# Two small float32 products of a fused attention and feed-forward kernel run as three passes of split operands

## The reference, cut to what matters

```python
z = x + x @ W.T + b            # for q, k1, k2, v1, v2, then split into 16 heads of 8
S1 = k1.T @ v1 / n ; S2 = k2.T @ v2 / n        # per batch and head, 8 x 8
out = (q @ S1 * mean(v2)) * g1 + rowsum(S1*S2) * g2 + (q @ S2 * mean(v1)) * g3 + (q @ (S1*S2)) * g4
x = layernorm(x + layernorm(out) @ Wo.T + bo)
x = layernorm(x + ffn_norm(x + relu(x @ w1 + b1) @ w2 + b2))
```

## Time and profile before

| what | value |
| --- | --- |
| median of 3 runs | 205.26 us (204.93 to 206.01) |
| profiled execution, its own time | 204.86 us |
| span of the profiled execution | 203.1 us |
| TensorE busy in the span | 191.3 us, 94% |
| VectorE busy | 157.7 us, 78% |
| GpSimd busy | 136.3 us, 67% |
| ScalarE busy | 129.2 us, 64% |
| mean granted TensorE clock | 0.991 of full speed |

### The profile page before, as it was taken

One profiled execution on the slowest core, in us unless ns is written; L12 is line 12 of the kernel. 1 busy time (PEld: TensorE's weight loads), 2 busy tenths in 40 slices (PEclk: granted clock), 3 DMA queues, 4 the chain that ended last, 5 costly groups with the idle time before them and its releaser, 6 DMA issues.

```text
span 203.1 us, 4279 instructions
## 1 busy us (share of the span) xinstructions
PE 191.3 (94%) x1375; PEld 174.7 (86%) x1375; DVE 157.7 (78%) x471; ACT 129.2 (64%) x386; POOL 136.3 (67%) x176
## 2 busy tenths in 40 slices
PE   6899999999999999999999999999999999999920
PEld 6788997999898999999997989898989899987820
DVE  0186745987879887898879896989698969897683
ACT  0342538373759665975858685967597759786852
POOL 8526670476489838986598759885988598877350
PEclk9999999999999999999999999999999999999996
DMA  5999501200001100101001400100010101011012
GB/s 149 247 230 283 154 0 32 52 0 5 0 0 52 48 6 2 56 0 52 3 14 50 118 4 0 53 24 31 2 52 5 52 3 52 2 52 38 17 53 103
DMA packets 12625, 10.64 MB, mean 52 GB/s; under 512 B 714, under 2 KB 10459, under 8 KB 12603
## 3 DMA queue, kind: packets, MB, share of 16 engines
q1 hardware_dynamic: 11944, 9.32, 15.3%
q0 software_dynamic: 352, 0.92, 2.4%
q10 hardware_dynamic: 306, 0.13, 0.2%
HBM read 6.17 MB, written 4.20 MB: 51 GB/s over the span
## 4 chain that ended last, share of the span: by engine, by line
PE 83%; DVE 6%; issue 3%; DMA 2%; ACT 2%; POOL 2%; DVEq 0%; POOLq 0%; SPq 0%; ACTq 0%
PE down_ps L997 25%; PE up_ps L997 24%; PE z_ps L997 14%; PE prep_ps L997 12%; PE turn_ps L1144 4%; PE turn_ps L1115 3%; DMA X<-in_L_attn_x 2%; DVE st L766 1%; DVE down_ps L817 1%; POOL y L528 1%; POOL y2g L524 1%; DVE z_ps L877 1%; DVE y2n L773 1%; ACT res L640 1%; DVE res L974 0%
## 5 line engine op out<-in xcount | busy, mean ns | idle before, releaser
L997 PE MATMUL down_ps<-w_sb,hT 128*128 128x128 f32 x480 | 58.9, 276 | 0.1
L997 PEld LDWEIGHTS down_ps<-w_sb,hT 128*128 128x128 f32 x480 | 56.4, 192 | 0.7 <-ACT hT L658 0.3
L658 ACT ACTIVATE hT<-up_ps,cols 128x512 f32<-128x512 f32 x64 | 42.3, 682 | 5.0 <-PE up_ps L997 4.7
L640 ACT ACTIVATE res<-y,nb,rstd 128x128 f32<-128x128 f32 x60 | 24.8, 483 | 6.6 <-POOL nb L510 5.9
L550 POOL TENSOR_TENSOR x1b<-x,b_rows 128x512 f32<-128x512 f32 x16 | 20.6, 1287 | 11.8 <-DVE x L773 11.8
L997 PE MATMUL up_ps<-x1T_hi,w_hi 128*128 128x512 f32 x64 | 26.1, 408 | 0.0
L997 PE MATMUL up_ps<-x1T_lo,w_hi 128*128 128x512 f32 x64 | 25.4, 398 | 0.0
L997 PE MATMUL up_ps<-x1T_hi,w_lo 128*128 128x512 f32 x64 | 25.3, 395 | 0.0
L524 POOL TENSOR_TENSOR y2g<-y2n,gamma_rows 128x512 f32<-128x512 f32 x15 | 19.3, 1285 | 8.1 <-DVE y2n L773 8.1
L773 DVE TENSOR_SCALAR x<-z_ps,st,rstd 128x128 f32<-128x128 f32 x64 | 21.9, 405 | 0.1
L607 ACT ACTIVATE z_sq<-z_ps 128x128 f32<-128x128 f32 x64 | 16.8, 270 | 8.1 <-PE z_ps L997 8.1
(11 more groups left out here) (160 smaller groups left out, 408.9 us busy)
## 6 DMA issues: line engine op xcount, KB each, us to landing
X<-in_L_attn_x SPq DMA_DIRECT2D x8, 512.0 KB, 8.8
out<-res SPq DMA_DIRECT2D x15, 256.0 KB, 2.0
V_all<-V_dram SPq DMA_DIRECT2D x6, 128.0 KB, 3.2
w_sb<-in_L_ffn_w POOLq DMA_DIRECT2D x2, 256.0 KB, 8.3
out<-res SPq DMA_DIRECT2D x2, 128.0 KB, 2.2
w_raw<-in_L_attn_Wv ACTq DMA_DIRECT2D x2, 64.0 KB, 2.6
w_raw<-in_L_attn_Wk SPq DMA_DIRECT2D x2, 64.0 KB, 3.8
w_raw<-in_L_attn_Wo POOLq DMA_DIRECT2D x1, 64.0 KB, 3.0
```

The lines of the kernel that those rows point to most:

```text
L640: last = act.activation(res[buf][:, t, :], y3[buf][:, t, :], ACT.Identity, scale=rstd4[:, t:t + 1], bias=nb4[:, t:t + 1])
L658: act.activation(hT[:, k, :], up_ps[k % len(up_ps)][:, :], ACT.Relu, bias=cols[:, 5 + k:6 + k]).then_inc(relu_out, 1)
L997: return pe.matmul(o, lhsT, rhs, start=start, stop=stop)
```

## The change

For batches 2 to 7 `gram_av` and `centered` no longer multiply float32 operands. Each operand is split into a high part in fp32r and its remainder in fp32r, and the product is the sum of high times high, high times low and low times high, three fp32r matmuls in one accumulation. So `gram_av(b)` has three matmul instructions where it had two, and `centered(b)` has six where it had four.

The constant sides are split once by GpSimd at the start of step 0 (`split_A`, `split_both`, two operations of 128 x 256 each). G of each batch is split by GpSimd at the end of the even steps 0 to 10, one step and more ahead of its use (`split_G`, two operations of 128 x 128). The high part of PT is what ScalarE's `PT_copy` now writes. The remainder is a new VectorE subtraction, `PT_rest`, that stands between the second and the third tile of x1 and waits for `PT_out`. `centered` waits for it (`PTlo_out`) before its first matmul.

```diff
@@ gpsimd
+            def split_both():
+                pool.wait_ge(zw_ready, 1)
+                pool.tensor_copy(both_hi[:, :, :], center[:, :, :]).then_inc(both_split, 1)
+                pool.wait_ge(both_split, 1)
+                pool.tensor_tensor(both_lo[:, :, :], center[:, :, :], both_hi[:, :, :].bitcast(f32), ALU.subtract).then_inc(both_split, 1)
+            def split_A():
+                pool.wait_ge(A_ready, 1)
+                pool.tensor_copy(A_hi[:, :, :], A_kv[:, 0:2, :]).then_inc(A_split, 1)
+                pool.wait_ge(A_split, 1)
+                pool.tensor_tensor(A_lo[:, :, :], A_kv[:, 0:2, :], A_hi[:, :, :].bitcast(f32), ALU.subtract).then_inc(A_split, 1)
+            def split_G(b):
+                g, k = b % 2, 2 * (b - 2)
+                pool.wait_ge(G_out, b + 1)
+                wait(pool, ev_done, b - 1)
+                pool.tensor_copy(G_hi[:, g, :], G_sb[:, b, 0:C]).then_inc(G_split, 1)
+                pool.wait_ge(G_split, k + 1)
+                pool.tensor_tensor(G_lo[:, g, :], G_sb[:, b, 0:C], G_hi[:, g, :].bitcast(f32), ALU.subtract).then_inc(G_split, 1)
             def body(st):
+                if st.n == 0:
+                    split_A()
+                    split_both()
...
+                if st.cur and n % 2 == 0 and n // 2 + 2 < BATCHES:
+                    split_G(n // 2 + 2)
@@ scalar, PT_copy
-                act.activation(PT_sb[:, :], prep_ps[:, 0:XW], ACT.Copy).then_inc(PT_out, 1)
+                act.activation(PT_sb[:, :] if b < 2 else PT_hi[:, :], prep_ps[:, 0:XW], ACT.Copy).then_inc(PT_out, 1)
@@ vector
+            def PT_rest(b):
+                wait(dve, PT_out, b + 1)
+                dve.tensor_tensor(PT_lo[:, :], prep_ps[:, 0:XW], PT_hi[:, :].bitcast(f32), ALU.subtract).then_inc(PTlo_out, 1)
-                    normalize(x1, y1_tile, st2, rstd2, x1_out)
+                    normalize(x1, y1_tile, st2, rstd2, x1_out, (lambda: PT_rest(st.prepared())) if st.prep and n >= 0 else None)
@@ tensor, gram_av, b >= 2
-                    mm(prep_ps[:, 0:256], G_sb[:, b, 0:C], A_kv[:, 0:2, :].rearrange("p j c -> p (j c)")).then_inc(ev_done, 1)
+                    if b == 2:
+                        pe.wait_ge(A_split, 2)
+                    wait(pe, G_split, 2 * (b - 1))
+                    hi, lo = (t[:, :, :].rearrange("p j c -> p (j c)") for t in (A_hi, A_lo))
+                    mm(prep_ps[:, 0:256], G_hi[:, b % 2, :], hi, start=True, stop=False)
+                    mm(prep_ps[:, 0:256], G_hi[:, b % 2, :], lo, start=False, stop=False)
+                    mm(prep_ps[:, 0:256], G_lo[:, b % 2, :], hi, start=False, stop=True).then_inc(ev_done, 1)
@@ tensor, centered
+                if b >= 2:
+                    wait(pe, PTlo_out, b - 1)
+                    pe.wait_ge(both_split, 2)
+                    hi, lo = (t[:, :, :].rearrange("p j c -> p (j c)") for t in (both_hi, both_lo))
+                    for part, pt in ((slice(0, 256), lambda t: t[:, 0:C]),
+                                     (slice(256, 512), lambda t: t[:, C:C + 1].to_broadcast([128, 128]))):
+                        mm(prep_ps[:, part], pt(PT_hi), hi, start=True, stop=False)
+                        mm(prep_ps[:, part], pt(PT_hi), lo, start=False, stop=False)
+                        last = mm(prep_ps[:, part], pt(PT_lo), hi, start=False, stop=True)
+                    last.then_inc(p_done, 1)
+                    return
```

More of the change, by code:

```diff
@@ L77, in build @@
         A_kv = sb("A_kv", [128, 5, 128])
+        A_hi = sb("A_hi", [128, 2, 128], f32r)
+        A_lo = sb("A_lo", [128, 2, 128], f32r)
+        G_hi = sb("G_hi", [128, 2, 128], f32r)
+        G_lo = sb("G_lo", [128, 2, 128], f32r)
         WoT = sb("WoT", [128, 128])
@@ L119, in build @@
         PT_sb = sb("PT_sb", [128, XW])
+        PT_hi = sb("PT_hi", [128, XW], f32r)
+        PT_lo = sb("PT_lo", [128, XW], f32r)
+        both_hi = sb("both_hi", [128, 2, 128], f32r)
+        both_lo = sb("both_lo", [128, 2, 128], f32r)
         PQ_hi = sb("PQ_hi", [128, 512], f32r)
@@ L227, in build @@
         rows_done = sem("rows_done")
+        both_split = sem("both_split")
+        PTlo_out = sem("PTlo_out")
+        A_split = sem("A_split")
+        G_split = sem("G_split")
         rows_out = sem("rows_out")
```

## The result

| | before | after |
| --- | --- | --- |
| median | 205.21 us (21 runs) | 205.68 us (21 runs) |
| ratio | | 1.0023, 95% interval 1.0014 to 1.0032 |
| span of the profiled execution | 203.1 us | 204.2 us |

The changed kernel is 0.47 us slower (0.29 to 0.66 by the interval). The forecast was 206.0 us, with "no change" as the likeliest class. The granted clock is the same in both profiles, 0.991 before and 0.992 after.

A forecast was written before the change was run, and what follows sets the result against it. TensorE's chain was taken as the bound: 1.02 us lost at `centered` (six times 0.17) less 0.24 saved at the product with G gives +0.78 us, 206.0 us on the median; range 204.7 to 207.0 us.

The forecast's parts named there:

- no change: Whole kernel: a time within about 0.5% (1.03 us) of before, between 204.2 and 206.3 us; chance 0.62.
- TensorE's chain is the bound, and `centered` starts the moment its input is there: At `centered`: its first load follows ScalarE's copy by 0.05 us, so waiting for PT_lo loses TensorE 0.33 us per batch.
- The rival that the wait is hidden: At `centered`: the remainder costs TensorE nothing, 1.2 us saved, 204.1 us; chance 0.12.
- The subtraction takes 0.30 us: `PT_rest` on VectorE: 130 columns take 0.30 us, by a line through 256 and 512 columns; bounds 0.16 and 0.425 us.
- the dearer remainder: Rival at `PT_rest`: the subtraction costs as much as one of 256 columns, 206.8 us; chance 0.18.
- the even case: Rival at `centered`: `PT_rest` takes near 0.16 us, so wait and saving even out, 205.2 us; chance 0.10.
- Three fp32r matmuls of 256 columns cost 0.354 us, six 0.71: Both products, at 0.118 us per matmul: `gram_av` saves 0.08 us per batch, `centered` 0.16 against float32's 0.87.
- the rival of slow spread loads: At `centered`: three matmuls loading the spread PT column cost 0.49 us more per batch, 208.9 us; chance 0.08.
- the estimate from the Trainium skill's four passes for true FP32: Both products: three passes cost three quarters of float32, saving 0.11 and 0.22 us per batch, sum +0.33 us; not adopted.
- the sum from the rows: Whole kernel: 1.02 us lost at `centered` less 0.24 saved at the product with G, +0.78 us.
- G's saving reaches the end in three batches of six: At `gram_av`: 0.08 us saved in batches 2 to 4, 0.24 in all; waits absorb it in 5 to 7.
- GpSimd hides its splits, VectorE's later x1 costs nothing: GpSimd's splits fit its idle gaps; x1's late tiles keep 1.3 us of cover, without which 0.5 us per batch.

The follow-up runs named there:

- the two kernels: Kernel before with only the subtraction and TensorE's wait added, all products float32: 207.33 us; changed kernel with the product with G back in float32: 206.01 us.
- the two halves of the change: Changed kernel with only the centered product split, 206.01 us, and with only the product with G split, 204.88 us.
- two pairs of kernels: Product with G split against float32: the changed kernel, 205.68 against 206.01 us; the kernel before, 204.88 against 205.30 us.
- rest_unwaited: Kernel before with the unread VectorE subtraction added and PT in its own bank, TensorE not waiting for the subtraction: 204.87 us, ratio 0.9986.
- rest_twice: Changed kernel with the subtraction done twice in a row on VectorE, the first into an unread tile: 206.81 us, 1.0077 of the kernel before.

## Why the prediction was right, step by step

*TensorE's chain is the bound, and `centered` starts the moment its input is there.* Right. The wait sits where it was put, and its 0.33 us per batch was measured by itself as 2.03 us in six batches. The rival that the wait is hidden is out: the load waits for PT_lo in all six batches, 0.33 to 0.34 us each.

*The subtraction takes 0.30 us.* The group rows of the kernel after, by form (busy us, mean ns, idle before):

```profile
L832 DVE TENSOR_TENSOR PT_lo<-prep_ps,PT_hi 128x130 fp32r<-128x130 f32 x6 | 1.8, 294 | 1.3 <-ACT PT_hi L668 0.9
L1043 PE MATMUL prep_ps<-both_hi,PT_lo 128*128 128x256 f32 x12 | 3.3, 279 | 0.0
```

294 ns. The line through the two wider rows held, which leaves neither the dearer remainder nor the even case standing.

*Three fp32r matmuls of 256 columns cost 0.354 us, six 0.71.* The matmuls of batch 2 after (57 to 60 us), and the first one behind them before (56.5 to 59 us):

```profile
58.33 0.38 PE L1043 MATMUL prep_ps<-both_hi,PT_hi 128*128 128x256 f32 x1
...
59.14 1.05 PE L1043 MATMUL down_ps<-w_sb,hT 128*128 128x128 f32 x8
```

```profile
58.59 0.61 PE L997 MATMUL down_ps<-w_sb,hT 128*128 128x128 f32 x4
```

From the first start to the start of what follows it is 0.81 us after, and 0.94 before (from 57.65). Both are more than the sum had (0.71 and 0.87), because the second matmul starts 0.22 us after the first instead of 0.118, and in float32 0.30 instead of 0.217. The saving is 0.13 us here and 0.15 by the two kernels, for a forecast of 0.16: nearly right. The chain's piece, 0.97 us for 0.95 before, doesn't show it: after the change it begins with the load that ends the wait, and before it began only when the record ahead ended, 0.16 us after the first matmul's start. One reading of the prediction was wrong without harm: 395 and 282 ns are the mean lengths of the float32 and the fp32r matmuls, not of a first and the later ones.

The fp32r matmuls follow one another at 0.11 to 0.12 us, and the spread column has no price in fp32r: its matmuls have the same 279 ns and the same spacing, and the two halves of the change sum to +0.90 us in the loop where the whole has +0.89. This settles the rival of slow spread loads. By the estimate from the Trainium skill's four passes for true FP32 ("FP8 and Floating Point Precision", TensorE Precision Notes) the loop would be +0.33 us. The loop is +0.89 and the sum from the rows was +0.78; the centered product saves 0.15 us per batch where the rows give 0.16 and that estimate 0.22. So the measurement goes with the rows.

*G's saving reaches the end in three batches of six.* Right, shown by two pairs of kernels (0.25 and 0.26 us). The waits, 48 to 180 us (us in total, times, longest), of the kernel before and then of the kernel after show why:

```profile
PEld prep_ps L997 <- DVE E_sb L827: 1.2, 3, 0.4
```

```profile
PEld prep_ps L1043 <- DVE PT_lo L832: 2.0, 6, 0.3
PEld prep_ps L1043 <- DVE E_sb L873: 1.5, 3, 0.6
```

There are three waits for E_sb, as before the change, and they are 0.3 us longer together: 0.07 us in each of batches 6 and 7, which is what G's product saved, and 0.18 in batch 5, where the gap named below comes on top.

*GpSimd hides its splits, VectorE's later x1 costs nothing.* Right. The timeline of POOL in the kernel after answers to the earlier trace rows:

```profile
130.49 0.29 POOL L543 CAST G_hi<-G_sb 128x128 fp32r<-128x128 f32 x1
130.86 0.46 POOL L545 TENSOR_TENSOR G_lo<-G_sb,G_hi 128x128 fp32r<-128x128 f32 x1
131.32 1.29 POOL L562 TENSOR_TENSOR y2g<-y2n,gamma_rows 128x512 f32<-128x512 f32 x1
...
134.78 0.20 POOL L519 TENSOR_TENSOR mr<-st,rstd 128x4 f32<-128x4 f32 x1 [0.81 <-DVE rstd L850]
```

The idle time before y2g is gone and the 0.8 us before mr is still there. That x1's delay is free was shown apart by rest_unwaited; it is 0.4 us, and the prediction had 0.5.

*What the sum missed.* The terms give +0.78 in the loop, where +0.89 was measured, and nothing elsewhere, where -0.32 was (25.84 us before and 25.52 after from the turn of x1 in step 13 to the end). Most of either comes from idle gaps of VectorE for which the trace names no other engine. The chain at the end of the kernel before, and of the kernel after:

```profile
192.96 1.28 POOL y L528
194.24 0.27 issue
194.52 0.09 DVE st L766
```

```profile
194.32 1.28 POOL y L566
195.60 0.02 issue
195.62 0.04 DVE st L807
```

VectorE starts 0.28 us after its input before, and 0.02 us after it in the changed kernel. Likewise, in batch 5, y2n starts 0.20 us after the start of the reciprocal ahead of it (116.67, 116.87) before, and 0.29 us after it (117.41, 117.70) in the changed kernel, which delays E_sb in a batch where TensorE waits for it. That batch takes 0.26 us more where 6 and 7 take 0.17 and 0.18. Loop plus end make +0.57 us for a measured +0.47 (0.29 to 0.66). The rest is within the interval; I have no cause for it and need none.

The two misses pull opposite ways. The first alone would have put the median 0.1 us above the forecast; the end of the kernel, which no term had, puts it 0.3 below. The mechanism was forecast, but that the two partly cancel is luck.

## What to carry to other kernels

Before an operand is split for cheaper passes, look at when its unsplit form is first used: where the consumer already starts 0.05 us after the producer, the remainder's own time is a new serial step, and it can cost more than the passes save (0.33 against 0.15 us here). Order the passes so that those with the high part run first and the remainder's come last, which may need a bank of its own; that turned +0.2% into -0.8% here, with the same number of instructions. Moving the whole product later only hands the wait on when what follows it has as little slack as what precedes it.

## What the runs showed of the hardware that I had not expected

The two gaps of VectorE go with the number of its instructions, in the twelve profiles of this study, one for each kernel. In batch 5 the distance is 0.20 us from the start of the reciprocal to that of y2n in the two kernels without `PT_rest`, 0.29 to 0.30 us in all nine with six operations more, and 0.20 us again with twelve more (rest_twice, one profile). The one near the end is there in those two kernels (0.28 and 0.27 us) and in none with six or twelve more. The trace names it issue and gives no releaser; that fetching of instructions makes it was not shown. An edit to one engine's program can so gain or lose 0.1 to 0.3 us at a place that it doesn't touch, and the larger figure is over half of what this change moved.
